# A two-layer graph network: early norms, a wait moved into a branch, and a reordered opening

## The reference

```python
h = jnp.maximum(_layernorm(x), 0.0)
support = jnp.matmul(h, W0)
x = x + segment_sum(support[src] * edge_weight[:, None], dst)

h = jnp.maximum(_layernorm(x), 0.0)
h1 = jnp.einsum('nd,od->no', h, W1) + b
# edges (src -> dst) and one self edge for every node
deg = zeros(n).at[row].add(1.0)
norm = deg[row] ** -0.5 * deg[col] ** -0.5
x = x + segment_sum(norm[:, None] * h1[col], row)
```

## Time and profile before

| | us |
|---|---|
| median of 3 runs | 1455.3 |
| lowest, highest | 1452.26, 1455.62 |
| the profiled execution | 1454.0 |
| its span, first to last instruction | 1452.2 |
| TensorE busy in the span | 1409.8 |
| VectorE, ScalarE, GpSimd busy | 914.0, 508.4, 465.3 |

### The profile page before, as it was taken

How to read it: one execution, slowest core, us unless ns; L and a number is a source line. 1 busy time by engine, 2 the same in 40 slices (tenths; PEclk the granted TensorE clock), 3 DMA queues, 4 the chain that set the end, 5 groups by cost and what they waited for, 6 DMA issues and landing times.

```text
span 1452.2 us, 23952 instructions
## 1 busy us (share of the span) xinstructions
PE 1409.8 (97%) x7586; PEld 844.2 (58%) x7587; DVE 914.0 (63%) x1818; ACT 508.4 (35%) x922; POOL 465.3 (32%) x851
## 2 busy tenths in 40 slices
PE   3999999999999999999999999879999999999999
PEld 2455555566667666666666665445456456456455
DVE  7897877827888966776876664772542542532532
ACT  7655655514545455554555434410000000000000
POOL 2256654515666755654655530000000000000000
PEclk9999999999999999999999999989999999999999
DMA  8305352352444545454536479919136037027002
GB/s 316 117 21 121 49 108 29 38 116 49 81 77 85 108 80 94 82 98 87 98 73 113 81 161 173 221 38 211 42 66 181 13 63 183 15 57 188 16 1 85
DMA packets 427819, 139.15 MB, mean 96 GB/s; under 512 B 397705, under 2 KB 409993, under 8 KB 427669
## 3 DMA queue, kind: packets, MB, share of 16 engines
q1 hardware_dynamic: 427669, 137.43, 44.3%
HBM read 53.46 MB, written 53.52 MB: 74 GB/s over the span
## 4 chain that ended last, share of the span: by engine, by line
PE 83%; issue 5%; SPq 4%; DVE 3%; POOL 2%; DMA 2%; ACT 1%; POOLq 0%; DVEq 0%; ACTq 0%
PE pair L1818 31%; PE pair L1906 20%; PE pair L1966 14%; PE pair L1705 11%; PE pair L1717 5%; SPq L587 3%; PE pair L1765 1%; PE pair L1688 1%; DVE own_w L1376 1%; DVE wmat L950 1%; DMA x_scratch<-xt 1%; SPq L592 1%; DMA slots<-c_scratch 1%; SPq L597 0%; DMA h<-in_x 0%
## 5 line engine op out<-in xcount | busy, mean ns | idle before, releaser
L1818 PE MATMUL pair<-h,area 128*128 128x512 f16 x2400 | 542.7, 379 | 0.0
L1818 PEld LDWEIGHTS pair<-h,area 128*128 128x128 f16 x2400 | 342.5, 146 | 147.6
L1906 PE MATMUL pair<-area,h 128*128 128x500 f16 x1600 | 340.0, 375 | 11.0 <-issue 11.0
L1906 PEld LDWEIGHTS pair<-area,h 128*128 128x128 f16 x1600 | 157.0, 98 | 193.2 <-issue 13.8
L789 POOL TENSOR_TENSOR deg_acc<-deg_acc,area 128x320 f32<-128x320 f32 x160 | 139.1, 869 | 246.8 <-DVE area L1130 244.8
L1966 PE MATMUL pair<-wmat,area 128*125 128x512 f16 x960 | 209.0, 379 | 0.0
L1639 ACT ACTIVATE area<-pair,sc 128x500 f16<-128x500 f32 x40 | 27.1, 677 | 444.4 <-PE pair L1906 444.4
L1436 ACT ACTIVATE area<-pair 128x320 f32<-128x320 f32 x160 | 70.1, 438 | 302.2 <-PE pair L1717 297.1
L1966 PEld LDWEIGHTS pair<-wmat,area 128*125 128x125 f16 x960 | 130.7, 137 | 75.5
L794 POOL TENSOR_TENSOR aux<-area,aux 128x320 f16<-128x320 f32 x144 | 147.8, 1027 | 0.0
L1443 ACT ACTIVATE aux<-area 128x320 f16<-128x320 f32 x144 | 126.5, 878 | 2.5 <-DVE area L1130 2.1
(11 more groups left out here) (210 smaller groups left out, 1268.3 us busy)
## 6 DMA issues: line engine op xcount, KB each, us to landing
c_scratch<-aux SPq DMA_DIRECT2D x72, 320.0 KB, 4.7
xt<-in_x SPq DMA_DIRECT2D x19, 512.0 KB, 3.6
x_scratch<-xt SPq DMA_DIRECT2D x19, 512.0 KB, 4.8
xt<-x_scratch SPq DMA_DIRECT2D x20, 448.0 KB
out_x<-xt SPq DMA_DIRECT2D x19, 448.0 KB
h<-x_scratch SPq DMA_DIRECT2D x4, 2048.0 KB, 8.4
h<-in_x SPq DMA_DIRECT2D x5, 1024.0 KB, 6.2
h<-in_L_gnn_W SPq DMA_DIRECT2D x4, 1024.0 KB, 11.1
```

Of the source, the lines that this page charges most:

```text
L1818: last = pe.matmul(sum_pair(e)[:, half * H:(half + 1) * H], wts(e)[:, q, :, k], hpart(k, r)[:, half * H:(half + 1) * H], start=k == q == r ...
L1906: ins = pe.matmul(sums_of(c, f), hpart(k, q)[:, f * P:(f + 1) * P], counts, start=first and q == 0, stop=last and q == 1, skip_group_check ...
```

## The change

Three things are changed.

In the second layer, VectorE makes the norm steps of the first twelve high parts between the splits of tiles 8 to 19, one behind each, and not all twenty behind the last split. Behind the last split stand the other eight, and then the ten steps on the `etab` half of the second parts, which stood behind the chunk's first evacuations before. The steps on the `slots` half take their place.

On TensorE, `second_halves` waits for the loads of the second parts inside the branch, where they are read, and no longer ahead of it. This holds for every chunk.

In the opening, VectorE makes the eight lower halves of W0 and the two scans first, and then `moments(1)` and `scale_shift(1)`. ScalarE does `field_out(1)` behind the second high half of W0 and not ahead of the first, and `std(1)` behind `field_out(3)` in tile 0. TensorE transposes tile 2 behind the sixth block of tile 1 and not behind the second.

```diff
             chain(nc.vector.tensor_scalar(unscale[:, 0:1], low[:, 2:3], wscale[:, 3:4], 1.0 / SUP_UP, ALU.mult, ALU.mult))
-            moments(1)
             for k in range(KD):
                 dve.wait_ge(w0_hi, k + 1)
                 nc.vector.scalar_tensor_tensor(wmat[:, 1, k, :], w_nat[:, k, :], scale_of[:, 2:3], wmat[:, 0, k, :],
                                                ALU.mult, ALU.subtract).then_inc(w0_lo, 1)
-                if k == 3:
-                    scale_shift(1)
             dve.wait_ge(rows_in, 32)
...
             nc.vector.tensor_tensor_scan(scans[:, NCH:2 * NCH], down, down, 1e9, ALU.min, ALU.min).then_inc(scans_ready, 1)
+            moments(1)
+            scale_shift(1)
...
             for t in range(7, T):
                 split(t)
+                if t >= KD:
+                    norms(0, t - KD, t - KD + 1, (ct_hi_of,))
...
-            norms(0, 0, T, (ct_hi_of,))
+            norms(0, T - KD, T, (ct_hi_of,))
+            norms(0, 0, LK, (ct_lo_of,))
             dve.wait_ge(dinv2_ready, 1)
...
                     sums2_left(c, f)
                     if c == 0:
-                        norms(c, f, f + 1, (ct_lo_of,))
+                        norms(c, LK + f, LK + f + 1, (ct_lo_of,))
                     elif step * f < T:
                         norms(c, min(T, step * f), min(T, step * (f + 1)))
                 if c == 0:
-                    norms(c, KD, T, (ct_lo_of,))
+                    norms(c, LK + KD, T, (ct_lo_of,))
...
             field_out(0)
-            field_out(1)
             act.wait_ge(w_pow, 1)
             for k in range(KD):
                 act.activation(wmat[:, 0, k, :], w_nat[:, k, :], ACT.Copy, scale=sc[:, 14:15]).then_inc(w0_hi, 1)
-                if k == 2:
-                    std(1)
+                if k == 1:
+                    field_out(1)
                 if k == 5:
                     field_out(2)
...
                 if t == 0:
                     field_out(3)
+                    std(1)
...
-                if t + 1 < T:
+                if t + 1 < T and t != 1:
                     transpose_rows(t + 1)
                 for k in range(2, KD):
                     support(t, k, k + 1)
+                    if t == 1 and k == 5:
+                        transpose_rows(t + 1)
...
             def second_halves(c, fs):
-                if 0 in fs:
+                with pe.If(most > EXACT):
                     for j in range(LJ):
                         pe.wait_ge(ctlo_in[j], 16 * (c + 1))
-                with pe.If(most > EXACT):
                     for f in fs:
```

More of the change, by code:

```diff
@@ L1321, in split, with norms @@
                 nc.vector.tensor_tensor(hpart(t, 1), h2_tmp(t), hpart(t, 0), ALU.subtract).then_inc(h2_ready, 1)
+            accs = [0]
+            def norms(c, k0, k1, parts=(ct_hi_of, ct_lo_of)):
+                for k in range(k0, k1):
+                    if k % HK == 0 and ct_hi_of in parts:
+                        dve.wait_ge(cthi_in[k // HK], 16 * (c + 1))
+                    if k % LK == 0 and ct_lo_of in parts:
+                        dve.wait_ge(ctlo_in[k // LK], 16 * (c + 1))
+                    for part_of in parts:
+                        counts = part_of(k)
+                        if accs[0] > 0:
+                            dve.wait_ge(acc_step, accs[0])
+                        accs[0] += 1
+                        if k == 0 and part_of is ct_hi_of:
+                            ins = nc.vector.tensor_scalar(s_acc, counts, dinv[:, 0:1], None, ALU.mult)
+                        else:
+                            ins = nc.vector.scalar_tensor_tensor(s_acc, counts, dinv[:, k:k + 1], s_acc,
+                                                                 ALU.mult, ALU.add)
+                        ins.then_inc(acc_step, 1)
+                if k1 == T and ct_lo_of in parts:
+                    dve.wait_ge(acc_step, accs[0])
+                    dve.sem_inc(acc_ready, 1)
             dve.wait_ge(stats_ready, T - 1)
```

21 lines of the change are left out of this document (removed).

## The result

The changed kernel takes 1443.48 us (median of five executions, 1442.64 to 1447.09), the kernel before, measured beside it, 1454.55 us (1452.26 to 1455.62). The ratio is 0.993, 95% interval 0.9913 to 0.9947. The forecast was 1444.0. A second measurement on another chip gave 1446.24 against 1457.04, ratio 0.9935 (0.9917 to 0.9952): the gain holds, but there single executions lay between 1444.56 and 1450.82. Where this scatter is from takes up much of what follows.

The account below looks back on a forecast made before the run. TensorE, busy 1409.8 of 1452.2 us, bounds the kernel, so only its gaps can be won: 10.9 us at the first chunk's sums plus 0.4 in the opening, 11.3 in all, giving 1444.0 us; eight times in ten 1441.5 to 1452.0.

Follow-up runs that it names:

- the kernel with idle DMA engines: Changed kernel with SP holding back second parts' transposes, bias and row loads until the first group of the last sums is done; 1453.13 us in one execution.

## What to carry over

A body that is never taken isn't free. A jump over 320 matmuls held TensorE's sequencer for 3.3 us at best and 8.7 at worst here; cut into 20 pieces among the work, each jump took 0.21 us (0.34 at most) ahead of the array and held nothing up. Two walls behind one another have to be moved together, and what a removed wait had covered (here the landing of rows for the last split) becomes the next bound, with its scatter. A lead over one profile of the kernel before should be measured from a landmark ahead of the edits, and held against more than one profile. A wait that a reordering creates should be priced with the clock, and one profile of a kernel doesn't show whether it falls.

## What was not expected of the hardware

- The price of a far jump has a part of 2.4 to 2.6 us behind its packet, nearly the same in nine of ten profiles (2.9 in the tenth), and one of 1.0 to 6.2 us ahead of it, shortest with the DMA engines idle.
- The granted clock fell after a stand of 2.45 us in one profile and held after 3.28 in another. In the kernel with idle DMA engines it fell at 944.0, when the engine had been at work again since 942.94, and in the opening at about 59, the engine at work since 57.33.
- The first split that waits for rows read back, measured from one and the same point of the program, moved by 3.4 us between two executions of one kernel, and by 4.8 over all profiles.
